# A fused attention and mixture-of-experts kernel: the context and the first weight ahead of the constants

## The reference

```python
q1, k1, v1 = heads(ln(x) @ Wq1), heads(ln(x) @ Wk1), heads(ln(x) @ Wv1)
q2, k2, v2 = heads(ctx @ Wq2), heads(ctx @ Wk2), heads(ctx @ Wv2)
out1 = softmax(q2 @ k1.T * SCALE) @ v1
out2 = softmax(q1 @ k2.T * SCALE) @ v2
alpha = sigmoid(alpha_attn)                      # one number
x = x + (out1 * alpha + out2 * (1 - alpha)) @ Wout + bout
h = ln(x)
p, i = top_k(softmax(h @ gate_w.T), 4);  p = p / sum(p)
x = x + sum_k p_k * ((silu(h @ w1[i_k]) * (h @ w3[i_k])) @ w2[i_k])
```

## Time and profile before

| | us |
|---|---|
| median of 3 runs (2071.16 to 2075.43) | 2072.59 |
| the profiled execution, its own time | 2074.48 |
| its span (first to last instruction) | 2072.7 |
| PE busy, of the span | 1856.4 (90%) |
| DVE busy | 1383.1 (67%) |
| ACT busy | 1249.7 (60%) |
| POOL busy | 1226.3 (59%) |

### The profile page before, as it was taken

One profiled execution on the slowest core, in us unless ns is written; L12 is line 12 of the kernel. 1 busy time (PEld: TensorE's weight loads), 2 busy tenths in 40 slices (PEclk: granted clock), 3 DMA queues, 4 the chain that ended last, 5 costly groups with the idle time before them and its releaser, 6 DMA issues.

```text
span 2072.7 us, 51812 instructions
## 1 busy us (share of the span) xinstructions
PE 1856.4 (90%) x15782; PEld 1646.2 (79%) x15783; DVE 1383.1 (67%) x3205; ACT 1249.7 (60%) x3605; POOL 1226.3 (59%) x1683
## 2 busy tenths in 40 slices
PE   5899999999999999999999999999749999999400
PEld 4788888888888888888888888888549999999300
DVE  4466776666776666677776677776656666666497
ACT  4676766666667666666766666766426666666200
POOL 2366666666666667666666666667536667667400
PEclk9899999999999999999999999999869999999755
DMA  3311111112111111111111111111568666666599
GB/s 115 107 55 60 51 46 46 59 49 71 47 51 46 49 51 54 51 36 41 36 44 41 54 36 41 36 41 39 161 193 263 186 190 192 183 189 184 197 410 353
DMA packets 159073, 215.06 MB, mean 104 GB/s; under 512 B 24481, under 2 KB 131633, under 8 KB 158769
## 3 DMA queue, kind: packets, MB, share of 16 engines
q1 hardware_dynamic: 123952, 132.08, 21.1%
q0 software_dynamic: 26112, 71.86, 9.4%
q10 hardware_dynamic: 8960, 10.52, 1.5%
HBM read 117.28 MB, written 101.38 MB: 105 GB/s over the span
## 4 chain that ended last, share of the span: by engine, by line
PE 76%; DMA 7%; DVE 5%; POOL 5%; issue 4%; ACT 2%; SPq 0%; DVEq 0%; POOLq 0%; ACTq 0%
PE p_av L1199 11%; PE p_pt L1179 10%; PE p_s L1162 10%; PE p_s L1103 9%; PE p_gu L1378 8%; PE p_x L1103 4%; PE p_y L1394 4%; PE p_x L1232 4%; DMA x_rows<-routed,slot_i 3%; DMA z<-mid_rows 3%; PE p_xt L1368 3%; PE p_s L1113 2%; PE p_av L1103 2%; PE p_pt L1103 2%; POOL y_rows L577 2%
## 5 line engine op out<-in xcount | busy, mean ns | idle before, releaser
L530 POOL TENSOR_TENSOR probs<-probs,inv 128x256 f32<-128x256 f32 x1024 | 597.5, 614 | 375.5 <-DVE inv L889 374.8
L635 ACT ACTIVATE probs<-p_s,nmx 128x256 f32<-128x256 f32 x1024 | 473.9, 484 | 59.7 <-PE p_pt L1179 41.7
L882 DVE TENSOR_REDUCE nmx<-p_s 128x4 f32<-128x1024 f32 x256 | 312.0, 1219 | 142.3 <-PE p_s L1162 142.3
L577 POOL DMA_INDIRECT y_rows<-y_out,xg x288 | 276.7, 961 | 147.1 <-issue 121.9
L522 POOL DMA_INDIRECT x_rows<-routed,slot_i x256 | 262.7, 1026 | 148.7 <-DVE target L874 86.0
L1179 PE MATMUL p_pt<-ident,probs 128*128 128x128 f32 x2048 | 292.6, 279 | 5.9 <-POOL probs L530 4.2
L1199 PE MATMUL p_av<-probsT,val 128*64 128x256 f32 x2048 | 256.2, 390 | 8.9 <-DVE probsT L777 6.2
L1179 PEld LDWEIGHTS p_pt<-ident,probs 128*128 128x128 f32 x2048 | 230.0, 142 | 39.2 <-issue 9.6
L623 ACT COPY probsT<-p_pt 128x512 f32<-128x512 f32 x256 | 151.3, 591 | 166.9 <-PE p_pt L1179 166.9
L635 ACT ACTIVATION_READ_ACCUMULATOR probs<-p_s,nmx 128x1 f32 x1024 | 219.6, 214 | 0.0
L1199 PEld LDWEIGHTS p_av<-probsT,val 128*64 128x64 f32 x2048 | 135.6, 138 | 85.2 <-issue 24.6
(11 more groups left out here) (194 smaller groups left out, 4997.4 us busy)
## 6 DMA issues: line engine op xcount, KB each, us to landing
xg<-x_rows SPq DMA_DIRECT2D x144, 257.0 KB, 3.6
y_in<-y_rows SPq DMA_DIRECT2D x32, 1024.0 KB, 9.6
rows<-in_ctx_dram SPq DMA_DIRECT2D x32, 256.0 KB, 2.7
x_in<-in_x_dram SPq DMA_DIRECT2D x32, 256.0 KB, 2.8
mid_rows<-x_mid SPq DMA_DIRECT2D x32, 256.0 KB, 2.2
y_rows<-y_out,xg POOLq DMA_INDIRECT x288
z<-mid_rows SPq DMA_DIRECT2D x17, 256.0 KB, 11.8
out_dram<-z ACTq DMA_DIRECT2D x17, 256.0 KB, 7.4
```

The costliest lines, as they stand in the source:

```text
L530: pool.tensor_tensor(pr[:, h, t, :], pr[:, h, t, :], rc[:, g:g + 1].to_broadcast([P, S]), ALU.mult).then_inc(normed_p, 1)
L577: pool.indirect_dma_start(y_rows, bass.IndirectOffsetOnAxis(ap=xg[r][:, i, D:D + 1].bitcast(I32), axis=0), y_out[r % 4][:, i, :], None).th ...
L635: act.activation(probs[u % 2][:, h, t, :], p_s[:, 2 * (u % 2) + h, t * S:(t + 1) * S], ACT.Exp, bias=nmx[u % 2][:, g:g + 1], accum_out=sum ...
L882: dve.tensor_reduce(nmx[i][:, :], p_s[:, 2 * i:2 * i + 2, :].rearrange("p h (t k) -> p (h t) k", t=ST), AX.X, ALU.max, negate=True).then_i ...
```

## The change

Every engine's program has its first part in another order, and some waits are narrower.

```diff
-        N_CONST = 3
+        N_CONST = 2
...
+        gate_bank = p_s[:, 2, 0:KT * E].rearrange("p (k e) -> p k e", k=KT)
...
             sp.dma_start(rows[:, :, :], ctx_dram[0]).then_inc(ctx_landed, 16)
-            sp.dma_start(gate_rows[:, :], gate_w).then_inc(const_in, 16)
-            sp.dma_start(bias[:, :], bout.rearrange("(a n) -> a n", a=1).to_broadcast([P, D])).then_inc(const_in, 16)
-            sp.dma_start(al[:, 0:1], alpha_attn.rearrange("(a n) -> a n", a=1).to_broadcast([P, 1])).then_inc(const_in, 16)
...
-            for n in range(EARLY):
-                if n == 4:
-                    sp.dma_start(x_in[:, :, :], x_dram[0]).then_inc(x_landed, 16)
+            load_piece(early, 0, early_in[0])
+            sp.dma_start(x_in[:, :, :], x_dram[0]).then_inc(x_landed, 16)
+            load_piece(early, 1, early_in[1])
+            sp.dma_start(gate_rows[:, :], gate_w).then_inc(gate_in, 16)
+            sp.dma_start(bias[:, :], bout.rearrange("(a n) -> a n", a=1).to_broadcast([P, D])).then_inc(const_in, 16)
+            sp.dma_start(al[:, 0:1], alpha_attn.rearrange("(a n) -> a n", a=1).to_broadcast([P, 1])).then_inc(const_in, 16)
+
+            for n in range(2, EARLY):
                 if n >= 4:
                     sp.wait_ge(early_lo, n - 3)
...
         def _(act):
-            act.wait_ge(const_in, 16 * N_CONST)
-
-            act.activation(al[:, 1:2], al[:, 0:1], ACT.Tanh, scale=0.5).then_inc(al_set, 1)
-            act.wait_ge(gate_t, 1)
-            act.copy(wgate[:, :, 0, :], p_x[:, 0:KT * E].rearrange("p (k e) -> p k e", k=KT)).then_inc(gate_hi, 1)
-            act.wait_ge(al_set, 3)
+            def constants():
+
+                act.wait_ge(gate_t, 1)
+                act.copy(wgate[:, :, 0, :], gate_bank).then_inc(gate_hi, 1)
+                act.wait_ge(const_in, 16 * N_CONST)
+                act.activation(al[:, 1:2], al[:, 0:1], ACT.Tanh, scale=0.5).then_inc(al_set, 1)
...
+                first = isinstance(b, int) and b < 0
+                if first:
+                    context_lo(0)
+                    early_rest(0)
                 if nxt:
                     dve.wait_ge(x_landed, 16 * (b + 2))
                     norm_stats(norm1(b + 1), x_in)
+                if nxt and not first:
                     context_lo(b + 1)
-                if isinstance(b, int) and b < 0:
-                    for m in range(3):
-                        early_rest(m)
+                if first:
+                    early_rest(1)
...
                     norm_apply(norm1(b + 1), x_in, lambda t: rows[:, t, :], ln1_set)
+                if first:
+                    early_rest(2)
...
-            pe.wait_ge(consts_set, 15)
-            pe.wait_ge(const_in, 16 * N_CONST)
-            for k in range(KT):
-                last = pe.transpose(p_x[:, k * E:(k + 1) * E], gate_rows[:, k * P:(k + 1) * P], ident[0:E, 0:E])
-            last.then_inc(gate_t, 1)
-
+
+            pe.wait_ge(consts_set, 5)
+
+            def gate_rows_t():
+
+                pe.wait_ge(gate_in, 16)
+                for k in range(KT):
+                    last = pe.transpose(gate_bank[:, k, :], gate_rows[:, k * P:(k + 1) * P], ident[0:E, 0:E])
+                last.then_inc(gate_t, 1)
```

More of the change, by code:

```diff
@@ L222, in xattn_moe_kernel @@
         wout_in = new("wout_in")
+        gate_in = new("gate_in")
         const_in, x_landed, ctx_landed, mid_stored, rows_sent, pads_sent = new(
@@ L393, in _ @@
         def _(sp):
-            sp.dma_start(rows[:, :, :], ctx_dram[0]).then_inc(ctx_landed, 16)
-            sp.dma_start(gate_rows[:, :], gate_w).then_inc(const_in, 16)
-            sp.dma_start(bias[:, :], bout.rearrange("(a n) -> a n", a=1).to_broadcast([P, D])).then_inc(const_in, 16)
-            sp.dma_start(al[:, 0:1], alpha_attn.rearrange("(a n) -> a n", a=1).to_broadcast([P, 1])).then_inc(const_in, 16)
             def load_piece(pieces, n, arrival):
@@ L401, in load_piece @@
                     sp.dma_start(dst, src).then_inc(arrival, 16)
-            for n in range(EARLY):
-                if n == 4:
-                    sp.dma_start(x_in[:, :, :], x_dram[0]).then_inc(x_landed, 16)
+            sp.dma_start(rows[:, :, :], ctx_dram[0]).then_inc(ctx_landed, 16)
+            load_piece(early, 0, early_in[0])
[5 more added lines that the diff above has]
+            for n in range(2, EARLY):
                 if n >= 4:
@@ L606, in value_evac @@
                 await_bank(b, n)
+                if isinstance(b, int) and b == 0:
+                    act.wait_ge(al_set, 3)
                 act.activation(val[d][:, n % 2, :], proj_bank(n), ACT.Copy,
@@ L697, in iteration @@
                     act.copy(flat(rowsT[1][0][:, :, :]), p_pt[:, 0, :]).then_inc(rowsT_hi, 1)
+                if isinstance(b, int) and b < 0:
+                    constants()
                 middle_piece(b, 0, 6)
@@ L765, in _, with constants @@
         def _(dve):
[L766 to L771, removed]
+            def constants():
+                dve.wait_ge(gate_hi, 1)
+                dve.tensor_tensor(wgate[:, :, 1, :], gate_bank, wgate[:, :, 0, :].bitcast(F32),
+                                  ALU.subtract).then_inc(gate_lo, 1)
+                dve.wait_ge(al_set, 1)
+                dve.tensor_scalar(alphas[:, 0:1], al[:, 1:2], 0.5, 0.5, ALU.mult, ALU.add).then_inc(al_set, 1)
+                dve.tensor_scalar(alphas[:, 1:2], al[:, 1:2], -0.5, 0.5, ALU.mult, ALU.add).then_inc(al_set, 1)
             dve.wait_ge(consts_set, 15)
@@ L1135, in project @@
                     wait(pe, attn_out, PAIRS * b)
+                elif n == 8 and isinstance(b, int) and b == 0:
+                    pe.wait_ge(gate_lo, 1)
+                    pe.wait_ge(consts_set, 15)
                 elif n == 11:
@@ L1205, in context_t @@
                 pe.wait_ge(ctx_landed, 16 * (b + 1))
-                if isinstance(b, int) and b == 0:
-                    pe.wait_ge(gate_lo, 1)
-                elif not isinstance(b, int) or b > 1:
+                if not isinstance(b, int) or b > 1:
                     pe.wait_ge(mid_set, b - 1)
@@ L1317, in iteration @@
                     probs_t(b, 3)
+                if isinstance(b, int) and b < 0:
+                    gate_rows_t()
                 if nxt:
```

## The result

The changed kernel takes 2066.63 us (median of 7 runs, 2063.0 to 2068.1) against 2073.23 us for the kernel before (7 runs, the three of the table above among them). The ratio is 0.9964 with a 95% interval of 0.9954 to 0.9974, so 5.4 to 9.5 us are gained. The forecast was 2066.0 us, with 6.7 us gained. One of the 22 runs of the kernel before that stand beside four of the experiments took 7085 us and is left out of their ratios.

A forecast was written before the change was run, and what follows sets the result against it. PE sets the body, so only the start, a chain of waits, can move. Projection 6 at 16.3 instead of 23.01 us gains 6.7, the clock 0: median 2072.6 becomes 2066.0 us, range 2061.5 to 2070.0.

The forecast's parts named there:

- the mark: Start of projection 6 on PE in the first batch: forecast at 16.3 instead of 23.01 us, all behind it gaining 6.7 us.
- The rival that the head start is given back: A later wait that does not move, such as batch 0's expert-weight loads, cancels the gain: 2072.6 us; chance 0.08.
- Wq2's arm: Start: Wq2 lands at 12.7 us, then its high part on ACT and low parts on DVE; projection 6 at 16.3.
- Alpha's arm: Start: alpha lands at 11.4 us, then POOL's `rstd`, normalised x, transposes to 14.1; covered by 0.1 to 0.2 us.
- the signs: Expected trace times: `rstd` after alpha at about 11.4, Wq2's high part at about 12.7, projection 2 at 7.7, projection 6 at 16.3.
- rival 1: Load queue: bias and alpha are hidden behind bulk loads, Wq2 lands by about 9; gain 9.3, 2063.3 us; chance 0.17.
- My cross-check: Load queue: same bytes in another order end at the same 14.2 us, Wq1 last, which puts Wq2 at 12.9.
- Term 0: TensorE's clock in projections 6 and 7: its 1.7 us loss is paid again, change 0, bounds 1.7 us gained or lost.
- Alpha at the queue's end: Load queue: alpha lands only at 14.2 us, projection 6 at 18.8; gain 4.2, 2068.4 us; chance 0.13.
- alpha later than 18.3 us: POOL's wait for alpha becomes the new stop, each us later costing one; 2079 us with alpha at 25; chance 0.03.

## Why the prediction was right

**How near, and by what.** The medians are 6.6 us apart where 6.7 was forecast, but the mark moved by 7.6 us between the first profiles and by 8.6 between the second. That the total agrees to 0.1 us is luck: the interval of the measurement is 5.4 to 9.5 us, and the forecast of the mark, a sum with two errors of opposite sign, was 0.9 us too low. What holds is the path: the start is a chain of waits, its gain passes on, and both the order of loads and that of the engines are needed.

**The mark and the bounds.** Everything behind projection 6 moved with it, as said: the second x 7.6 us earlier, `x_res` too (36.01 against 43.63 us). The rival that the head start is given back didn't come true; three spans of after are 2066.3, 2063.9 and 2062.5 us against 2072.7 and 2071.5. One number was loose: 45.2 us for a batch holds for the first 16 in which the padding is filled; later ones take 44.5.

**The arms.** "Wq2's arm", with projection 6 coming 3.6 us behind Wq2, was right in mechanism and size: 15.11 - 11.43 = 3.68 and 15.28 - 11.65 = 3.63. "Alpha's arm" close behind it was right too; in two profiles of three `rstd` waited for alpha. In the first profile the statistics came later still, because Wk2 landed at 6.6 us and stands ahead of them on DVE, and because `rstd` took 1.55. That arm I had put 2 us lower. Of the signs, `rstd` at 10.26 and Wq2's high part at 11.41 are within the 2 us allowed, and projections 6 and 7 took less than 6 us together in every profile; but in the first profile `rstd` was ended by DVE's statistics, not by alpha, and projection 2 began at 9.1, 8.7 and 8.8 us in the three instead of 7.7.

**The terms that were mis-sized**, with opposite signs:
- The bulk loads. The sum let them land at the full rate of 395 GB/s: Wk2 4.8, x 5.5, Wk1 6.8. They landed at 5.1 to 6.6, 5.8 to 7.2 and 8.1 to 8.6. In 7 to 9 us of the first profile the engines moved only 132 GB/s.

```profile
7.00:9.00 2.00, 0.20 (x2) 0.20 (x2) 1.34 (x2) 1.05 (x2) 0.00 (x0) 1.00 0.37 132
```

- Bias and alpha. The sum shifted their whole price by 3.3 us: alpha 11.4, Wq2 12.7, so 5.9 us between Wk1 (6.8) and Wq2. Measured are 10.0 and 11.4, and 2.8 us between Wk1 (8.6) and Wq2, 3.3 and 3.2 in the other two profiles, of which Wq2 itself needs 1.3. Behind bulk loads the bias landed 0 to 1.1 us after Wk1. That is a part of rival 1, whose full form (Wq2 by 9) did not come true; taking both away from there brought Wq2 to 9.8 and 9.6.
- My cross-check, that the same bytes end at the same 14.2 us, was wrong for the same reason: Wq1 landed at 4.78 + 7.9 = 12.7 us.
- The gate rows were to land at 6.8 and be no stop. They landed at 8.3 to 8.8, and PE waited for them, ahead of projection 2. Projection 2 then took 2.9 us where the sum had 2.6. Neither reached projection 6 here, since other arms ended later; both did once those were shorter.

Wq2's arm alone, with Wq2 1.3 us earlier than forecast, would have put projection 6 at 15.0. In the first profile the late Wk2 and the long `rstd` gave 0.4 us of that back. That makes 15.4 instead of 16.3.

**The clock.** Term 0 was right for the first profile (4.60 us for projections 6 and 7, 4.61 before), and its bounds were needed. In the third profile the chain is longer there:

```profile
15.55 2.90 PE p_x L1126 x12
18.45 2.56 PE p_av L1126 x12
21.01 3.21 PE p_s L1126 x24
```

The 48 matmuls take 8.67 us instead of 7.49, 1.2 us lost, inside the bound of 1.7. TensorE was at half speed for longer, which no row ahead of it tells: the transposes of x ahead of it took 1.12 us, but they took 1.11 in the second profile too, whose 48 matmuls needed 7.49 us.

**The rivals.** Alpha at the queue's end (2068.4) and alpha later than 18.3 us (slower) didn't happen: alpha took 6.2 to 6.3 us from its issue, 5.9 before. The range of 2061.5 to 2070.0 holds the result and all three profiled executions of the changed kernel.

## What to carry to other kernels

Find the first instruction that the steady work waits for, and follow each engine back from it: a constant that is needed late but waited for early, on any engine or ahead on the load queue, holds the whole start. Move the load and the waits together; one without the other gave about a quarter of the gain. A start that is shifted by some us in a kernel whose loop waits only for itself keeps its gain to the end, but a loop that scatters by 1 to 3 us (785.6 to 788.9 us here, for one kernel) hides differences of that size in a few runs. The mark in the trace shows them where the timing doesn't, if it is read from more than one profile: it scattered by 0.4 and 0.7 us itself.

## What the runs showed of the hardware

- **A repeated read is dear.** Loading one row of 1 KB to 128 partitions landed 4.1 us after its issue, 128 different rows 2.4 us; one number of 4 bytes to 128 partitions took 5.9 us behind the former, 3.2 behind the latter, and 2.3 us as different numbers behind the latter. Everything behind in the queue waited: Wk2 landed at 9.5, 7.5 and 7.1 us in the three cases.
- **DVE holds POOL.** `rstd` took 1.55 us in 10.26 to 11.81 when DVE's Wk1 step with two inputs in SBUF had begun at 10.01, and 0.72 when `rstd` began first (9.06 and 9.09) or DVE was idle. In between, the third profile of the changed kernel shows 1.25 us:
```profile
10.24 1.25 POOL L522 TENSOR_TENSOR rstd<-ve,mhalf 128x2 f32<-128x2 f32 x1 [4.62 <-DMA al<-_L_xattn_alpha_attn_dram]
```
```profile
9.69 1.22 DVE L911 SCALAR_TENSOR_TENSOR wp_lo<-probs,wp_hi 128x1024 fp32r<-128x1024 f32 x1
```

In all four profiles where DVE's step began first (three of the changed kernel, one of the engines' order alone), `rstd` ended 0.57 to 0.58 us behind that step's end, whenever it had begun. The Trainium skill, "SBUF — State Buffer", section "Who interferes with whom", says that such a DVE instruction and a GpSimd one that reads SBUF contend for a shared interface, and that the one that starts first holds the other up. The rows agree where DVE starts first; where `rstd` did, DVE's step took 1.24 us instead of 1.22, so the other direction does not show for so short an instruction.
- **The clock column can be high while matmuls are slow.** In the third profile of the changed kernel the granted clock reads 1.00 in 17 to 18 us, with 6 matmuls in 1 us:

```profile
17.00:18.00 1.00, 1.00 (x6) 1.00 (x6) 0.00 (x0) 0.00 (x0) 0.00 (x0) 1.00 1.07 335
```

At full speed 10 or 11 stand in such a row. It isn't peculiar to that profile: in the kernel before, projection 2 has 7 matmuls in 18 to 19 us, and 12 in 2.92 us, with 1.00 in the column. The spacing of matmuls is the safer sign of the clock.
